# Mixture-of-experts stage with tiles of 256 rows instead of 512, bias rows by SyncE's transfers, and part of VectorE's work on ScalarE

## The reference

```python
mla_out = ao @ o_w + o_b                      # ao: attention, only 128 of 256 columns not zero
probs = softmax(mla_out @ router_w + router_b)
topw, topi = top_k(probs, 2)                  # each row goes to 2 of 8 experts
topw = topw / (topw.sum(-1) + 1e-08)
h1 = gelu(einsum('bsd,edf->ebsf', mla_out, w1) + b1)   # 256 -> 512
h2 = einsum('ebsf,efd->ebsd', h1, w2) + b2             # 512 -> 256
moe_out = einsum('bse,ebsd->bsd', combine, h2)
return hs + 0.3 * moe_out
```

## Time and profile before

| | before |
|---|---|
| time, median of 3 | 4210.51 us (4210.18 to 4212.61) |
| the profiled execution | 4181.01 us |
| its span | 4179.4 us |
| TensorE busy | 3521.1 us, 84% |
| VectorE busy | 3303.0 us, 79% |
| ScalarE busy | 2306.6 us, 55% |
| GpSimd busy | 1369.6 us, 33% |
| mean granted clock of TensorE | 0.918 |

### The profile page before, as it was taken

The page is one execution under the profiler, slowest core; times in us unless marked ns, Lnnn a source line. Parts: engine busy times, 40 slices in busy tenths (PEclk is TensorE's granted clock), DMA queues, the critical chain, the costliest instruction groups (busy, mean ns, idle before and its releaser), DMA issues. The chain is left out here.

```text
span 4179.4 us, 65579 instructions
## 1 busy us (share of the span) xinstructions
PE 3521.1 (84%) x20079; PEld 2113.7 (51%) x20080; DVE 3303.0 (79%) x4251; ACT 2306.6 (55%) x4128; POOL 1369.6 (33%) x905
## 2 busy tenths in 40 slices
PE   8968888889557979978699999999999995479950
PEld 3445555555346868877433333333333334379950
DVE  8959999999786656545789889898898956668868
ACT  6755555555594533310068888888888881123333
POOL 4448888889203444400100000000000003745530
PEclk9989999999888989989689999999999995589985
DMA  6665444444577943367213232323222204323349
GB/s 218 249 206 176 162 162 165 167 165 143 201 258 194 243 112 105 92 170 201 81 27 74 52 73 52 73 53 70 56 65 60 52 8 132 116 76 91 91 159 292
DMA packets 534915, 537.05 MB, mean 128 GB/s; under 512 B 85168, under 2 KB 440624, under 8 KB 534496
## 3 DMA queue, kind: packets, MB, share of 16 engines
q1 hardware_dynamic: 520704, 496.18, 40.7%
q0 software_dynamic: 13952, 37.74, 2.7%
HBM read 317.41 MB, written 215.19 MB: 127 GB/s over the span
## 5 line engine op out<-in xcount | busy, mean ns | idle before, releaser
L2321 DVE TENSOR_REDUCE at_top<-at_psM 128x1 f32<-128x1024 f32 x1024 | 1206.1, 1220 | 136.5 <-PE at_psM L2172 135.7
L2281 ACT ACTIVATE at_probs<-at_psS 128x512 f32<-128x512 f32 x2048 | 1060.9, 603 | 250.9 <-PE at_psS L2198 250.9
L2198 PE MATMUL at_psS<-at_q,at_k 64*128 64x512 f32 x2048 | 795.4, 468 | 8.3 <-ACT at_probs L2281 8.3
L575 POOL TENSOR_TENSOR sc_prod<-sc_state,sc_c_row 128x1024 f32<-128x1024 f32 x256 | 709.0, 2789 | 117.1 <-DVE sc_state L724 105.8
L2172 PE MATMUL at_psM<-at_k,at_q 62*128 62x512 f32 x2048 | 689.2, 451 | 36.5 <-DMA at_vraw<-scratch_vf 21.9
L724 DVE TENSOR_TENSOR_SCAN sc_state<-sc_dec,sc_psI 128x1024 f32<-128x1024 f32 x256 | 578.4, 2280 | 53.2 <-PE sc_psI L645 29.4
L2172 PEld LDWEIGHTS at_psM<-at_k,at_q 62*128 62x128 f32 x2048 | 312.9, 190 | 602.1 <-DVE at_top L2321 519.9
L2211 PE MATMUL at_psV<-at_probs,at_v 128*32 128x512 f32 x4096 | 546.4, 605 | 0.0
L656 PE MATMUL sc_psY<-sc_prod,sc_ident 128*128 128x512 f32 x1024 | 467.6, 597 | 3.5 <-DVE sc_y L710 2.2
L606 ACT ACTIVATE sc_dec<-sc_dt,sc_a_exp 128x1024 f32<-128x1024 f32 x256 | 293.5, 1147 | 311.3 <-DVE sc_state L724 308.6
L2198 PEld LDWEIGHTS at_psS<-at_q,at_k 64*128 64x128 f32 x2048 | 337.6, 184 | 195.4 <-ACT at_probs L2281 190.8
(11 more groups left out here) (393 smaller groups left out, 5013.2 us busy)
## 6 DMA issues: line engine op xcount, KB each, us to landing
sc_c_row<-scratch_bc SPq DMA_DIRECT2D x128, 512.0 KB, 4.2
scratch_xs<-at_zeros SPq DMA_DIRECT2D x140, 264.0 KB, 4.9
sc_b_row<-scratch_bc SPq DMA_DIRECT2D x64, 512.0 KB, 5.2
ec_y<-scratch_ys SPq DMA_DIRECT2D x32, 512.0 KB, 6.8
ex_x<-scratch_xs SPq DMA_DIRECT2D x39, 264.0 KB, 3.3
si_x<-in_x SPq DMA_DIRECT2D x16, 512.0 KB, 4.4
scratch_xn<-si_xn SPq DMA_DIRECT2D x16, 512.0 KB, 5.1
scratch_x_t<-si_xT SPq DMA_DIRECT2D x16, 512.0 KB, 5.7
```

The source lines that it names most:

```text
L575: pool.tensor_tensor(prod[:, (n * H + h) % 8, :], state[slot][:], c_row[n % ROWS][:], ALU.mult).then_inc(prod_ready, 1)
L2198: pe.matmul(psS[v % 3][:], rows_of(k4[j], h, 0, GROUP)[:, c * P:(c + 1) * P], rows_of(q4[j], h, 0, GROUP)[:, half * TILE:(half + 1) * TILE ...
L2281: act.activation(probs[:, slot(j, v), :], psS[v % 3][:], ACT.Exp).then_inc(act_done, 1)
L2321: dve.tensor_reduce(top[j % 2][:, h, c:c + 1], psM[t % 2][:], AX.X, ALU.max, negate=True).then_inc(maxed, 1)
```

## The change

All of it is in `compute`, with two small consequences in `route`.

1. The experts' tiles have ETILE = 256 rows (2 groups of 128) instead of 512, so TILES is 71. All buffers of the stage shrink with it; `route` makes its tile table for 71 tiles. Each step now works on 256 rows; y is made, and its scatter started, once a tile, and `psY` alternates by tile instead of by half.
2. The bias of a tile's expert no longer comes from `K.b2`. SyncE transfers the expert's one row, spread over the partitions, into `b2[par]` (128 KB) for every tile: `bias(i + 2)` in step i, behind `load(i + 3)`; two are issued ahead of the first load. It waits for `y_ready`, since `collect` reads the buffer. The transfer of `K.b2` in `route` goes.
3. ScalarE copies the tile's w1 (`first_weights(i + 2)`, at the end of its step) and the head of the second half of the hidden values (after the four Gelus). VectorE did both.
4. VectorE's step is in another order: the small slot operations stand singly between the large ones (`unused`, `numbered`, `placed`, `names`).

The core of the diff (left out: shapes of buffers, the start of the loops, renamed arguments):

```diff
-TILES = 2 * N // TILE + E - 1
+ETILE = 2 * P
+ESUB = ETILE // P
+TILES = 2 * N // ETILE + E - 1
...
-                sp.dma_start(flat(K.b2[:]), spread(A["b2"].rearrange("e d -> (e d)"), E * D)).then_inc(late, 16)
-                sp.wait_ge(late, 16)
...
+                def bias(i, par):
+                    later(sp, y_ready, i - 1)
+                    m.settle(sp)
+                    e = sp.value_load(K.tile_expert[0:1, bass.ds(i, 1)], min_val=0, max_val=E - 1)
+                    sp.dma_start(b2[par][:], A["b2"].rearrange("e (a d) -> e a d", a=1)[bass.ds(e, 1), :, :].to_broadcast([P, 1, D])).then_inc(b2_loaded[par], 16)
 
                 def step(i, par, ahead):
                     if ahead >= 3:
                         load(i + 3, 1 - par)
+                    if ahead >= 2:
+                        bias(i + 2, par)
+                bias(0, 0)
+                bias(1, 1)
                 load(0, 0)
                 load(1, 1)
                 load(2, 0)
...
+                def first_weights(i, par):
+                    e = expert(i)
+                    for part in two:
+                        src = K.w1[part][:].rearrange("p e f -> p (e f)")[:, bass.ds(e * FF, FF)]
+                        act.activation(w1[par][part][:], src.bitcast(F32), ACT.Copy).then_inc(w1_ready, 1)
 
                 def hidden(i, par):
                     e = expert(i)
                     later(act, hid_rest, 2 * (i - 1))
-                    later(act, out_psum, 2 * (i - 1))
+                    later(act, out_psum, i - 1)
                     for f in range(FT):
                         act.wait_ge(hid_psum, FT * i + (f + 1))
-                        act.activation(whole[par][:, f, :], psH[f][:], ACT.Gelu,
+                        act.activation(whole[par][:, f, :], psH[f][:, 0:ETILE], ACT.Gelu,
                                        bias=K.b1[:, bass.ds(e * FT + f, 1)]).then_inc(hid_ready, 1)
+                    act.wait_ge(hid_ready, FT * i + FT)
+                    act.activation(hid[par][0][:, 2:4, :], whole[par][:, 2:4, :], ACT.Copy).then_inc(hid_other, 1)
 
                 def step(i, par, ahead):
                     if ahead >= 2:
                         turn_head(i + 2, par)
                     if ahead >= 1:
                         hidden(i + 1, 1 - par)
+                    if ahead >= 2:
+                        first_weights(i + 2, par)
...
-                    for half in two:
-                        later(pe, y_ready, 2 * (i - 1) + (half + 1))
...
+                    later(pe, y_ready, i - 1)
+                    for n in range(ESUB):
+                        ss = slice(n * P, (n + 1) * P)
+                        for f in range(FT):
...
                 def collect(i, par):
+                    dve.wait_ge(out_psum, i + 1)
+                    dve.wait_ge(b2_loaded[par], (i - par) * 8 + 16)
+                    dve.tensor_tensor(y[par][:], psY[par][:], b2[par][:].to_broadcast([P, ESUB, D]), ALU.add).then_inc(y_ready, 1)
 
                 def step(i, par, ahead):
-                    place(i, par)
+                    unused(i, par)
                     if ahead >= 2:
-                        dve.wait_ge(slot_ready, i + 1)
-                        front(i + 2, par)
+                        rest_of_rows(i + 2, par)
+                    numbered(i, par)
                     if ahead >= 1:
-                        divide(i + 1, 1 - par)
+                        first_head(i + 1, 1 - par)
+                    placed(i, par)
+                    if ahead >= 2:
+                        dve.wait_ge(padded, 3 * i + 3)
+                        names(i + 2, par)
+                    if ahead >= 1:
+                        dve.wait_ge(hid_head, i + 2)
+                        rest_of(i + 1, 1 - par, 0)
+                        dve.wait_ge(hid_other, i + 2)
+                        rest_of(i + 1, 1 - par, 1)
                     collect(i, par)
```

More of the change, by code:

```diff
@@ L2653, in _ @@
                 then(dve.tensor_tensor(start[:], tilenum[:], start[:], ALU.subtract))
-                then(dve.scalar_tensor_tensor(out=start[:], in0=which[:], scalar=float(N // TILE), in1=start[:],
+                then(dve.scalar_tensor_tensor(out=start[:], in0=which[:], scalar=float(N // ETILE), in1=start[:],
                                               op0=ALU.mult, op1=ALU.add))
@@ L2733, in store @@
                     pool.wait_ge(slot_ready, i + 1)
-                    for half in two:
[L2735 to L2740, removed]
+                    pool.wait_ge(y_ready, i + 1)
+                    m.settle(pool)
+                    for s in range(ESUB):
+                        pool.indirect_dma_start(
+                            out=A["ys"], out_offset=bass.IndirectOffsetOnAxis(ap=slot[par][:, s:s + 1], axis=0),
+                            in_=y[par][:, s, :], in_offset=None).then_inc(y_st[par], 16)
                 identity(nc, pool, ident, made)
                 for k in two:
-                    pool.iota(spare[k][:], pattern=[[P, SUB]], base=1 + 2 * N + k * TILE, channel_multiplier=1,
+                    pool.iota(spare[k][:], pattern=[[P, ESUB]], base=1 + 2 * N + k * ETILE, channel_multiplier=1,
                               allow_small_or_imprecise_dtypes=True).then_inc(made, 1)
@@ L2786, in turn @@
                     later(pe, x_rest, i)
-                    for s in range(SUB):
-                        last = pe.transpose(psT[:, s, :], x[par][:, s, 0:P], ident[:])
+                    for s in range(ESUB):
+                        last = pe.transpose(psT[:, s * P:(s + 1) * P], x[par][:, s, 0:P], ident[:])
                     last.then_inc(turned, 1)
@@ L2803, in output @@
                     pe.wait_ge(hid_rest, 2 * i + 2)
-                    for half in two:
-                        later(pe, y_ready, 2 * (i - 1) + (half + 1))
[L2806 to L2810, removed]
-                                last = products(pe, psY[half][:, n, :], ((xh, wh), (xh, wl), (xl, wh)), f == 0, f == FT - 1)
-                        last.then_inc(out_psum, 1)
+                    later(pe, y_ready, i - 1)
+                    for n in range(ESUB):
+                        ss = slice(n * P, (n + 1) * P)
+                        for f in range(FT):
+                            xh, xl = (hid[par][part][:, f, ss] for part in two)
+                            wh, wl = (weight[part][:, bass.ds(e * FT + f, 1), :] for part in two)
+                            last = products(pe, psY[par][:, n, :], ((xh, wh), (xh, wl), (xl, wh)), f == 0, f == FT - 1)
+                    last.then_inc(out_psum, 1)
                 def step(i, par, ahead):
@@ L2855, in place @@
                     dve.tensor_tensor(slot[par][:], pad[:, 2, :], pad[:, 1, :], ALU.add).then_inc(slot_ready, 1)
-                def divide(i, par):
-                    for half in two:
-                        fs = slice(2 * half, 2 * half + 2)
-                        head, rest = (hid[par][part][:, fs, :] for part in two)
-                        dve.wait_ge(hid_ready, FT * i + 2 * half + 2)
-                        dve.tensor_copy(head, whole[par][:, fs, :]).then_inc(hid_head, 1)
-                        dve.wait_ge(hid_head, 2 * i + half + 1)
-                        dve.tensor_tensor(rest, whole[par][:, fs, :], head.bitcast(F32), ALU.subtract).then_inc(hid_rest, 1)
@@ L2866, in collect, with first_head @@
-                def collect(i, par):
-                    e = expert(i)
-                    for half in two:
-                        dve.wait_ge(out_psum, 2 * i + half + 1)
-                        bias = K.b2[:, bass.ds(e, 1), :].to_broadcast([P, 2, D])
-                        dve.tensor_tensor(y[par][:, 2 * half:2 * half + 2, :], psY[half][:], bias, ALU.add).then_inc(y_ready, 1)
+                def first_head(i, par):
+                    dve.wait_ge(hid_ready, FT * i + 2)
+                    dve.tensor_copy(hid[par][0][:, 0:2, :], whole[par][:, 0:2, :]).then_inc(hid_head, 1)
```

73 lines of the change are left out of this document (43 added, 30 removed).

## The result

The changed kernel took 4276.53 us (median of 4 runs, 4269.07 to 4280.65) against 4211.56 us for the kernel before (4 runs, 4210.18 to 4215.05): ratio 1.0148, interval 1.0135 to 1.0161. Forecast were 4236 us and a range up to 4262. The direction was right, the size was not: +65 us instead of +26.

What follows compares the result with a forecast made beforehand. TensorE alone bound the stage before; afterwards SyncE's loop would, at 5.13 us a tile. Loop +21.7, start +1 and clock +3 made +25.7 us, taking the median from 4210.5 to 4236 us, range 4207 to 4262.

Steps and rivals of the forecast that it cites:

- From one transfer instruction to the next with a read between, no wait: 1.23: SyncE's queue: the load of x goes out 1.23 us after the bias row.
- P = 4.38: TensorE's own work on one tile of 256 rows, transposes, hidden and output layer together: 4.38 us.
- the change offers: The `compute` stage: if TensorE stayed the bound, 307.6 us against 336.2, a gain of 28.6 us.
- 0.4 us to spare; cost nothing while SyncE's loop is the cover: ScalarE's weight copies: ready 4.9 us after the transposes, asked for by TensorE's hidden layer at 5.3, so no cost.
- if that loop were gone ... 0.1 to 0.4: ScalarE's weight copies: without SyncE's loop, asked for at 4.56 us and costing some 0.1 to 0.4.
- Landing 2.8: The half-size load of x: 2.8 us from issue to landing, bounds 2.4 and 3.3.
- Clock, +3: TensorE, busy 85% in short pieces, runs partly at half rate: +3 us, bounds 0 and +12.
- Start, +1: Start of the stage: first output 0.7 us earlier, TensorE longer at 1.2 GHz, net +1 us.
- the second: Rival: the load is on time and TensorE or ScalarE binds, 4.38 to 4.55 us a tile, 4187 us; chance 0.09.
- The third: Rival: SyncE's loop is short, landing 2.3 and both SyncE steps 0.2 faster, 4210 to 4218 us; chance 0.09.
- The fourth: Rival: a second chain on top (late weights or rests), or the clock low for long, 4262 to 4300 us; chance 0.09.
- the first: The forecast itself: SyncE's loop, with x's load behind the wait for y, binds; 4236 us, 4218 to 4258; chance 0.73.

Runs made afterwards that it cites:

- e1: The changed kernel with the biases kept in SBUF as before, so SyncE's queue holds only the x loads: 4201.2 us, ratio 0.9986.
- e2: The changed kernel with the same bias transfers issued one step later, waiting for the collect before: 4208.2 us, ratio 0.9994.
- e4: The changed kernel with GpSimd filling an unused buffer ahead of each tile's two scatters, which moves them later: 4250.2 us, ratio 1.0096.
- e3: The changed kernel with SyncE's loop written out for all 71 tiles, no branch between bias row and next load: 4238.9 us, ratio 1.0065.
- e6: e1 with the weight copies back on VectorE, behind the rest of x: 4189.2 us, ratio 0.9942.
- e10: e2 with the weight copies on VectorE, as in e6: 4191.8 us, ratio 0.9953.
- e5: e1 with ScalarE's two weight copies a tile moved ahead of the four Gelus: 4195.3 us, ratio 0.9959.
- e7: The kernel before, tiles of 512 rows, with only the bias rows transferred by SyncE in the changed kernel's queue order: 4219.1 us, ratio 1.0018.

## Why the prediction was wrong

The mechanism that was forecast is the one that ran: the load of x stands on SyncE's queue behind a wait for y, e1 takes the slow-down away by leaving the bias rows out, and e2 by moving their wait alone. The size was not right, and one step has most of the error. In the loop that sets the pace (the one whose bias row is followed by the turn of SyncE's loop) the two tiles take 11.76 us where 10.26 were forecast:

| term | forecast | measured |
|---|---|---|
| y addition | 0.69 | 0.69 |
| end of y to bias row | 0.96 | 0.88 |
| bias row to load of x | 1.23 | 2.67 |
| load to transposes | 2.8 | 2.29 |
| transposes to the y that closes the loop | 4.58 | 5.23 |

- **"From one transfer instruction to the next with a read between, no wait: 1.23"** is the step that failed, by 1.44 us. The row was read at the start of the stage, where GpSimd scatters nothing and no loop turns. In the steady loop the scatter of the same y is released by the same semaphore as the bias row and runs beside SyncE's reads. By e4, 1.06 us of the 2.67 is the stall under the scatter and 0.33 the turn of the loop. e3 and e4 each give back 38 to 42 us of the stage, the clock's part included.
- **P = 4.38** was 0.15 too small as TensorE's own pace: e6 and e10 show 4.53 without a gap. 12 hidden matmuls take 1.51, not 1.40, and 24 output matmuls 2.88, not 2.80. So the 28.6 us that "the change offers" were 18 (336.2 to 318.4).
- **ScalarE's "0.4 us to spare; cost nothing while SyncE's loop is the cover"**: the spare time failed, since the two loops did not settle at even distances. In the short interval of 5.05 us or less the weights are late, as the passage above shows (0.43 us, released by ex_w). The cost held: this wait falls into the other loop, ahead of a wait for x; in the loop that sets the pace the hidden layer starts 0.26 us behind the transposes, with no wait for weights. And "if that loop were gone ... 0.1 to 0.4" held too: e5 gives 0.16 us a tile, e6 0.27.
- **Landing 2.8** was too long by 0.5. The Trainium skill (DMA: Bandwidth & Descriptors, section "Anatomy of one DMA"), with 2.0 us fixed and the rest by bytes, gave 2.3 for the half load. The section fits this rule to transfers that GpSimd issues, while these are SyncE's, which the prediction did not say. The trace has 2.29, from the transfer instruction to the transposes: here the rule was nearer than my halving of the row. For the load of 264 KB it had been under the row (2.6 against 3.3).
- **Clock, +3**: it cost some 12 us, at the upper bound. The granted clock is 0.95 to 0.97 in the steady part, between the 0.98 and 0.93 taken from the earlier trace rows, but the loss falls on the loop that sets the pace. In 8 of its 31 passes (transposes of the odd tiles 9 to 69) the matmuls from the first of the hidden to the last of the output layer take 5.7 to 5.8 us, in the other 23 4.3. One of the 8 and the tile behind it (timeline, TensorE), then the same stretches with the granted clock, 0.72 as a mean and 1.00, the upper level:

```profile
3757.17 0.43 PE L2811 MATMUL ex_psT<-ex_ident,ex_x 128*128 128x128 f32 x2 [1.98 <-DMA ex_x<-scratch_xs]
3757.39 2.66 PE L2354 MATMUL ex_psH<-ex_xT,ex_w 128*128 128x256 f32 x12
3759.85 3.61 PE L2354 MATMUL ex_psY<-ek_w,ex_hid 128*128 x24
3763.30 0.38 PE L2811 MATMUL ex_psT<-ex_ident,ex_x 128*128 128x128 f32 x2
3763.43 1.67 PE L2354 MATMUL ex_psH<-ex_xT,ex_w 128*128 128x256 f32 x12
```

```profile
3757.30:3763.30 6.00, 6.00 (x39) 5.98 (x38) 2.35 (x7) 4.00 (x8) 1.43 (x2) 0.72 0.28 88
3763.40:3768.00 4.60, 4.58 (x39) 4.38 (x37) 3.28 (x10) 3.29 (x8) 2.47 (x2) 1.00 0.16 53
```

  TensorE had idled for 1.7 to 2.3 us ahead of the 8 and for 1.0 to 2.0 us ahead of the others. So of the 0.65 us by which the last line of the table is over, some 0.36 is the clock and the rest TensorE's pace at full clock.
- **VectorE**, **GpSimd** and **routing: 0** held in that none is a bound. VectorE's 3.8 us a tile was too much: it is busy for 138.9 of 250 us, 3.3 a tile. "The slot operations set between large ones: 0" held for the changed kernel, whose bound is elsewhere; in e6, where VectorE is at 86%, they are worth 6 us.
- **Start, +1**: -1.0.

Per tile 0.75 us more than forecast (half of 11.76 - 10.26), times 67, is 50 us: 21.7 + 50 = 72, the 72.5 measured in the stage. Of the 50, the gap between bias row and load makes 48, TensorE's pace and the clock 22, and the earlier bias row and landing take 20 back.

Of the rivals, the second (TensorE binds, 4187 us) needed a chain shorter by 1.5 us; e2 and e10 shorten it by issuing the bias row a step later, and e10 reaches 4192, at the 4.53 us a tile that the rival names. The third had the landing right (2.3) and the steps on SyncE the wrong way: together they are 3.55 us (0.88 + 2.67), where it wanted 1.8. The fourth names the time that came (4262 to 4300), but not its cause: neither the weights nor the rests set the pace. Only its clock is a part of it, 12 us; the rest is a longer step in the chain of the first.

## What to carry to other kernels

A queue issues in order: before a wait is put on it, write down which instructions stand behind it and when each is needed, in tiles. Halving the tile halves the time that such a chain has, but not its fixed parts (reads, issue, landing), so an order that cost 5 us of the stage at 8.8 us a tile became the bound where TensorE needs 4.5. Take the price of a step on a queue from its steady loop, with what the other queues do at that moment, and not from the start of the stage. And read an engine's own pace from a version without waits: at a busy share of 99%, e1 was still 0.27 us a tile above it.

## What the runs showed of the hardware

- **SyncE's register work stalls while GpSimd issues an indirect transfer.** The read of the tile's place on SyncE in the kernel before (its first profile), in the changed kernel, and in e4 (count, min/median/max ns):

```profile
L2718 SPq TENSOR_LOAD <-ek_tile_at x39: 263/307/495, 3676.5 to 3992.6; - x39
```

```profile
L2720 SPq TENSOR_LOAD <-ek_tile_at x71: 5/268/715, 3706.9 to 4111.1; - x71
```

```profile
L2721 SPq TENSOR_LOAD <-ek_tile_at x71: 16/268/282, 3713.2 to 4080.7; - x71
```

  By the records of the traces, 40 of SyncE's register instructions in the changed kernel take 600 to 800 ns, and all 40 lie over a scatter of GpSimd, though the scatters fill a third of the time; in e3 13 (13 over a scatter), in e7 65 (62), in e4, where they are moved apart, none. Those of the changed kernel end 0.7 or 1.45 us after a scatter's start. In e10 there are 23, each over a scatter, and they cost nothing, since no load stands behind a wait there. What SyncE and GpSimd share was not tried.
- **The same matmul at two paces.** Before, output matmuls start 0.117 us apart (5.49 us for 47 steps); in e6 and e10, with the same shape and a granted clock of 1.00, 0.120 (2.76 for 23). Whether it comes from the shorter stretch of hidden matmuls ahead of them stays open.
- **A stretch without a change of its own can differ by 30 us.** `route` took 215.6 us in one execution of the kernel before, 247.7 in another, and 242 to 249 us in all other profiles. The cause stays open.
